# Expert weights split tile by tile inside the attention loop, padding rows written by plain transfers

## The chip, the cores and the metric

The kernel runs on one core of a Trainium2 chip. The metric is the time of one execution on the device in microseconds (us), taken as the median of the runs. TensorE is called PE, VectorE DVE, ScalarE ACT, GpSimd POOL and SyncE SP, as in the profile. SP does nothing here but issue transfers.

## What is computed

One decoder layer on x, 2048 rows by 256 columns, all in float32:

```python
x = x + attn(_layernorm(x))      # one head of width 256; scores q A q^T / 16, softmax, times v, times the row's norm
x = x + xattn(_layernorm(x), ctx, mask)   # 4 heads of 64, 1601 context rows
x = x + ffn(_layernorm(x))       # 4 experts of 256 -> 1024 -> 256 with exact GELU

idx = argmax(softmax(x @ Wg + bg))        # each row goes to one expert
out = gelu(x @ W1[idx] + b1[idx]) @ W2[idx] + b2[idx]
```

## The kernel before

**Precision.** Each float32 operand of a large product is held as a high half (rounded to the matmul's type) and a low half (the rest), and three matmuls (high by high, high by low, low by high) replace one. ACT makes the high half by a copy, DVE the low half by a subtraction (`low`, line 1316). Nearly every PSUM tile in the kernel goes through such a pair. The expert weights W1 and W2 (4 MB each) need it too.

**Prologue** (to about 95 us): keys and values of both attentions are made and stay in SBUF, in `keys_self`, `vals_self`, `keys_cross` and `vals_cross`.

**Attention loop.** The 2048 rows are T = 16 tiles of 128 rows. All engines run the same pipelined pass `body(j, k)`, 18 times (`run_pipeline`, line 400): in pass j, part a works on the self-attention of tile j, part b on the first cross-attention heads of tile j-1, and part c on the last heads, the output projection, the gate and the routing of tile j-2. Passes 3 to 14 are one hardware loop; passes 0 to 2 and 15 to 17 are written out. Pass 16 (k = T) has no part a, and pass 17 (k = T+1) has only part c. The order within each engine is written by hand in `body`, and semaphores tie the engines together. PE's three PSUM banks for transposes are handed from one use to the next in a fixed order.

**Routing.** For each tile DVE finds the expert and the place of every row (`gates`, `ranks`, `destination`), and POOL scatters the tile's records (256 columns and the row's number) into `rows_dram` by an indirect transfer (line 631). `rows_dram` has one region of 2048 + 128 records for each expert. Expert blocks are 128 records, so behind the last record of each expert there must be padding records. In pass 17, after `pad_rows` (line 1657, DVE) has worked out where each expert's records end so far, POOL issues eight indirect transfers of 128 padding records each (lines 599 to 607), two for each expert, and the last record scatter waits for them (line 630).

**Weights.** After the last x1 SP loads W1 and then W2, in eight pieces of 1 MB, through two halves of `w_stage` (lines 486 to 501). ACT makes the high half (`weights_hi`, line 1145) and DVE the low half (`weights_lo`, line 1451) of each piece, four of them in pass 16, two in pass 17, and two behind it. `w1s` and `w2s` lie in SBUF where the keys and values lay, so none of it can begin before those are done with.

**Experts.** DVE works out a table of the 19 blocks, which says for each where its rows and weights lie (lines 1721 to 1744). Then SP loads 128 records (`load_rows`), DVE and POOL normalise them, PE multiplies with W1, DVE adds b1, ACT applies GELU, PE multiplies with W2, DVE adds b2 and x, and POOL scatters the rows to the output, 19 times (`blocks`). Columns of the weights are chosen by a register loaded from the table.

Of the kernel before, what the change touches and what calls it, by code (L numbers as in the profile page):

```python
# [46 lines left out]
NOBODY = 65536.0  # L47

# [29 lines left out]
def emit(nc, io, ctx):  # L78
# [8 lines left out]
    rows_dram = nc.dram_tensor("rows_dram", [XROWS, REC], F32, kind="Internal").ap()  # L87

# [29 lines left out]
    pad_f = sb("pad_f", [P, 2, E], F32)  # L118
    pad_i = sb("pad_i", [P, 2, E], U32)
# [3 lines left out]
    tab = sb("tab", [P, 5, BLOCKS], F32)  # L123
    table = sb("table", [P, 3, BLOCKS], I32)
# [71 lines left out]
    ps_self = sb("ps_self", [P, 4, 2, 512], F32R, loop)  # L196
# [10 lines left out]
    o_tile = sb("o_tile", [P, H, HD], F32, loop)  # L207
    ot = sb("ot", [P, 2, C, P], F32R, loop)
    xn3 = sb("xn3", [P, D], F32, loop)
    x3t = sb("x3t", [P, C, P], F32, loop)  # L210
# [139 lines left out]
    pad_dest = sem("pad_dest")  # L350
    pad_dest_i = sem("pad_dest_i")
# [3 lines left out]
    w_loaded = [sem("w_loaded_even"), sem("w_loaded_odd")]  # L355
    b_loaded = sem("b_loaded")
    w_hi = sem("w_hi")
    w_lo = sem("w_lo")
# [62 lines left out]
    def _(sp):  # L421
# [42 lines left out]

        loads_a(0)
# [15 lines left out]

        sp.wait_ge(x1_ready, T)
        for n in range(2 * E):
            e = n % E
            if n >= 2:
                sp.wait_ge(w_hi, n - 1)
                sp.wait_ge(w_lo, n - 1)  # L490
            if n < E:
                sp.dma_start(w_stage[:, n % 2, :].rearrange("p (c n) -> p c n", c=C),
                             io["W1"][e].rearrange("(c p) n -> p c n", p=P)).then_inc(w_loaded[n % 2], 16)
            else:
                sp.dma_start(w_stage[:, n % 2, :].rearrange("p (c n) -> p c n", c=FC),
                             io["W2"][e].rearrange("(c p) n -> p c n", p=P)).then_inc(w_loaded[n % 2], 16)
            if n == E + 1:

                sp.wait_ge(cross_p_used, 16 * T)
                sp.dma_start(b2_row[:, :], bass.AP(io["b2"].tensor, 0, [[0, P], [1, E * D]])).then_inc(b_loaded, 16)  # L500
                sp.dma_start(b1_row[:, :], bass.AP(io["b1"].tensor, 0, [[0, P], [1, E * DF]])).then_inc(b_loaded, 16)

        sp.wait_ge(spare_stored, 16 * E)
        sp.wait_ge(routed, 16 * T)
        sp.wait_ge(table_ready, 3)
# [23 lines left out]
    def _(pool):  # L529
# [50 lines left out]
        def body(j, k):  # L580
# [18 lines left out]
            if k == T + 1:  # L599


                for n in range(2):
                    for e in range(E):
                        pool.wait_ge(pad_dest_i, 1)
                        pool.indirect_dma_start(out=rows_dram[:, :],  # L605
                                                out_offset=bass.IndirectOffsetOnAxis(ap=pad_i[:, n, e:e + 1], axis=0),
                                                in_=pads[:, :], in_offset=None).then_inc(pads_out, 16)
# [12 lines left out]
            if c:  # L620
# [8 lines left out]
                if k == T + 1:  # L629
                    pool.wait_ge(pads_out, 16 * 2 * E)  # L630
# [35 lines left out]
    def _(pe):  # L666
# [99 lines left out]
        def self_values(j, k, g):  # L766
            pe.wait_ge(self_p_lo, 4 * j + g + 1)
            for n in range(4):
                m = 4 * g + n
                for a, b in ((0, 0), (0, 1), (1, 0)):  # L770
                    mm = pe.matmul(self_out[:, 0:D], ps_self[:, g, a, n * P:(n + 1) * P], vals_self[:, m, b, :],  # L771
# [255 lines left out]
        pe.wait_ge(table_ready, 3)  # L1027
# [8 lines left out]
        def blocks(b, k):  # L1036
# [10 lines left out]
            if k < BLOCKS:  # L1047
                if k == 0:
                    pe.wait_ge(w_lo, E)
                pe.wait_ge(f_xt_lo, b + 1)  # L1050
                off = pe.value_load(table[0:1, 1, bass.ds(b, 1)], min_val=0, max_val=(E - 1) * DF)
                for n in range(2):
                    three(scores[:, n, :], lambda a, c: xt_f[:, a, c, :],
                          lambda p, c: w1s[:, p, c, bass.ds(off + n * 512, 512)]).then_inc(f_h, 1)
            if k < BLOCKS - 1:
                flip_x(b + 1, k + 1)
            if k >= 1:
                if k == 1:
                    pe.wait_ge(w_lo, 2 * E)
                off2 = pe.value_load(table[0:1, 2, bass.ds(b - 1, 1)], min_val=0, max_val=(E - 1) * D)  # L1060
                if k >= 2:
                    pe.wait_ge(f_out, b - 1)
                for f in range(FC):
                    if f % 4 == 0:
                        pe.wait_ge(f_ht_lo, 2 * (b - 1) + f // 4 + 1)
                    for a, p in ((0, 0), (0, 1), (1, 0)):
                        mm = pe.matmul(cross_out[:, 0:D], ht[:, a, f, :], w2s[:, p, f, bass.ds(off2, D)],  # L1067
# [6 lines left out]
    def _(act):  # L1074
# [70 lines left out]
        def weights_hi(n):  # L1145

            e = n % E
            act.wait_ge(w_loaded[n % 2], 16 * (n // 2 + 1))
            if n < E:
                copy(w1s[:, 0, :, e * DF:(e + 1) * DF], w_stage[:, n % 2, :].rearrange("p (c n) -> p c n", c=C)).then_inc(w_hi, 1)  # L1150
# [23 lines left out]
        def body(j, k):  # L1174
# [11 lines left out]
            if k == T:  # L1186
                weights_hi(0)
# [669 lines left out]
```

## Time and profile before

| | us |
|---|---|
| three runs | 841.83, 843.74, 843.75 |
| median | 843.74 |
| span of the profiled execution | 848.8 |
| its time outside the span | not shown by the profile |
| PE busy in the span | 755.1 (89%) |
| DVE | 653.2 (77%) |
| ACT | 457.9 (54%) |
| POOL | 138.9 (16%) |

The span is the time from the first to the last instruction of one profiled execution; it is 5 us longer than the median of the runs without a profile. Busy time of an engine is the sum of its instructions' times. A wait is shown as idle time in front of an instruction, with the one whose signal ended it. The granted clock of PE is given as a share of 2.4 GHz, so 1.00 is 2.4 and 0.50 is 1.2 GHz. In the profile a line such as L1318 can be that of a helper: L1318 is every low half, L1076 every copy on ACT. The loop's passes are 33.9 us apart. The drain passes 16 and 17 lie at 620 to 662 and 662 to 694 us, and the expert blocks from 700 us to the end, 6.73 us apart.

### The profile page before, as it was taken

What the parts mean: (1) busy time and instruction counts of PE and PEld (TensorE: products, weight loads), DVE (VectorE), ACT (ScalarE), POOL (GpSimd) and SP (SyncE); (2) the same over time, 40 slices, a digit from 0 to 9 for tenths busy, and PEclk for the clock granted to TensorE, in tenths of its full rate; (3) what the DMA queues carried; (4) which work ended last, traced back from release to release, by engine and by line L of the source; (5) the groups of instructions that cost most, each with busy time, mean ns of one, the idle gap of its engine ahead of it and who ended that gap; (6) DMA issues with size and microseconds to landing.
All of it is one profiled execution on the core that took longest, in us unless ns stands there. A gap on an engine that the chain in (4) does not pass through costs nothing. (4 is left out here: it accounts for less than half of the span.)

```text
span 848.8 us, 19493 instructions
## 1 busy us (share of the span) xinstructions
PE 755.1 (89%) x6136; PEld 681.1 (80%) x6137; DVE 653.2 (77%) x1619; ACT 457.9 (54%) x922; POOL 138.9 (16%) x246
## 2 busy tenths in 40 slices
PE   3988799999999999999999999999986416999996
PEld 2778689989889899898898998988975314999995
DVE  5984647788888888888888888888878465777773
ACT  2544626566566665666666656666665432334332
POOL 3100110120211201202112012021120410222221
PEclk9999989999999999999999999999978856999999
DMA  6242110010101000000010000000123260111110
GB/s 211 70 138 70 47 29 7 24 29 15 29 12 28 28 6 28 24 16 28 12 28 28 6 28 24 17 28 12 54 113 99 101 235 26 36 39 39 37 33 15
DMA packets 25525, 39.32 MB, mean 46 GB/s; under 512 B 3086, under 2 KB 18704, under 8 KB 25360
## 3 DMA queue, kind: packets, MB, share of 16 engines
q1 hardware_dynamic: 23232, 33.02, 12.5%
q0 software_dynamic: 2256, 5.83, 2.0%
q8 instruction: 21, 0.34, 0.2%
q14 instruction: 16, 0.13, 0.0%
HBM read 28.82 MB, written 10.41 MB: 46 GB/s over the span
## 5 line engine op out<-in xcount | busy, mean ns | idle before, releaser
L1076 ACT ACTIVATE ps_cross<-flip 128x512 f16<-128x512 f32 (+1 forms) x256 | 125.0, 514 | 116.5 <-PE flip L795 91.0
L1318 DVE TENSOR_TENSOR ps_cross<-flip,ps_cross 128x512 f16<-128x512 f32 (+1 forms) x256 | 145.0, 583 | 24.8 <-ACT ps_cross L1076 20.4
L795 PE MATMUL flip<-ident,exp_cross 128*128 128x128 f32 (+1 forms) x832 | 131.8, 282 | 9.9 <-DVE ps_cross L1318 6.5
L1277 ACT ACTIVATE exp_cross<-exp_cross,xneg 128x1024 f32<-128x1024 f32 (+1 forms) x128 | 122.7, 960 | 19.2 <-DVE xneg L1492 19.1
L784 PE MATMUL scores<-keys_cross,qt 128*128 128x402 f32 x512 | 127.6, 372 | 5.3 <-DVE xneg L1492 3.5
L795 PEld LDWEIGHTS flip<-ident,exp_cross 128*128 128x128 f32 (+1 forms) x832 | 95.8, 143 | 18.1 <-DVE ps_cross L1318 8.3
L672 PE MATMUL scores<-keys_self,u_tile 128*128 128x512 f32 x384 | 102.2, 403 | 6.4 <-issue 4.9
L806 PE MATMUL cross_out<-vals_cross,ps_cross 128*128 128x128 f16 (+1 forms) x832 | 102.5, 224 | 5.5 <-issue 4.9
L771 PE MATMUL flip<-vals_self,ps_self 128*128 128x256 f32 x768 | 103.8, 289 | 0.0
L806 PEld LDWEIGHTS cross_out<-vals_cross,ps_cross 128*128 128x128 f16 (+1 forms) x832 | 76.4, 101 | 28.3 <-issue 20.4
L771 PEld LDWEIGHTS flip<-vals_self,ps_self 128*128 128x128 f32 x768 | 96.7, 194 | 0.0
L808 PE MATMUL cross_out<-vals_cross,ps_cross 128*128 128x64 f16 (+1 forms) x832 | 95.6, 195 | 0.0
L784 PEld LDWEIGHTS scores<-keys_cross,qt 128*128 128x128 f32 x512 | 87.4, 193 | 5.8 <-DVE xneg L1492 3.6
L672 PEld LDWEIGHTS scores<-keys_self,u_tile 128*128 128x128 f32 x384 | 67.6, 188 | 19.2 <-issue 6.0
L808 PEld LDWEIGHTS cross_out<-vals_cross,ps_cross 128*128 128x128 f16 (+1 forms) x832 | 75.1, 100 | 1.1
L1492 DVE CUSTOM_DVE_ANT_0 exp_cross<-scores,mask_bias,xneg 128x804 f32<-128x804 f32 x64 | 67.3, 1052 | 7.5 <-PE scores L784 4.2
L1492 DVE CUSTOM_DVE_ANT_0 exp_cross<-scores,mask_bias 128x804 f32<-128x804 f32 x64 | 63.3, 988 | 4.2 <-PE scores L784 2.6
L672 PE MATMUL scores<-w1s,xt_f 128*128 x228 | 61.6, 421 | 2.4 <-issue 2.4
L1067 PE MATMUL cross_out<-w2s,ht 128*128 x456 | 58.2, 284 | 1.2 <-DVE ht L1318 1.2
L1067 PEld LDWEIGHTS cross_out<-w2s,ht 128*128 128x128 f32 x456 | 54.9, 189 | 1.5 <-issue 1.4
L672 PEld LDWEIGHTS scores<-w1s,xt_f 128*128 128x128 f32 x228 | 43.9, 200 | 12.6 <-issue 3.0
L1076 ACT ACTIVATE ps_self<-flip 128x512 fp32r<-128x512 f32 x64 | 38.6, 605 | 28.3 <-PE flip L763 28.2
(207 smaller groups left out, 1189.2 us busy)
## 6 DMA issues: line engine op xcount, KB each, us to landing
w_stage<-W SPq DMA_DIRECT2D x8, 1024.0 KB, 5.4
u_dram<-u_out SPq DMA_DIRECT2D x4, 1024.0 KB, 5.9
u_tile<-u_dram SPq DMA_DIRECT2D x16, 256.0 KB, 2.7
mask_tile<-mask SPq DMA_DIRECT2D x16, 200.1 KB, 2.4
rows<-rows_dram SPq DMA_DIRECT2D x19, 130.0 KB, 2.1
x_all<-x SPq DMA_DIRECT2D x4, 512.0 KB, 5.8
x_tile<-x SPq DMA_DIRECT2D x16, 128.0 KB, 2.0
b_row<-b SPq DMA_DIRECT2D x1, 2048.0 KB, 8.9
```

What stands on the lines that cost most here:

```text
L672: mm = pe.matmul(out, lhs(a, c), rhs(b, c), start=(n == 0 and first), stop=(n == 3 * C - 1 and last))
L771: mm = pe.matmul(self_out[:, 0:D], ps_self[:, g, a, n * P:(n + 1) * P], vals_self[:, m, b, :], start=(m == 0 and a == 0 and b == 0), stop= ...
L784: mm = pe.matmul(scores[:, n, 0:KB], qt[:, h, :], keys_cross[:, part, h, n * KB:(n + 1) * KB], start=(part == 0), stop=(part == 1))
L795: tr = pe.transpose(flip[0:rows, bank(use), n * P:(n + 1) * P], exp_cross[:, h % 2, m * P:m * P + rows], ident[:, :])
L806: pe.matmul(cross_out[:, h * P:(h + 1) * P], ps_cross[0:rows, g, 0, n * P:(n + 1) * P], vals_cross[0:rows, m, h, :, :], start=(m == 0), st ...
L808: mm = pe.matmul(cross_out[:, h * P:h * P + HD], ps_cross[0:rows, g, 1, n * P:(n + 1) * P], vals_cross[0:rows, m, h, 0, :], start=False, s ...
L1067: mm = pe.matmul(cross_out[:, 0:D], ht[:, a, f, :], w2s[:, p, f, bass.ds(off2, D)], start=(f == 0 and a == 0 and p == 0), stop=(f == FC - ...
L1076: return act.activation(out, in_, ACT.Copy, **kw)
L1277: act.activation(exp_cross[:, h % 2, cols], exp_cross[:, h % 2, cols], ACT.Exp, bias=xneg[:, h % 2, 1:2], scale=-1.0, accum_out=xden[:, ha ...
L1318: return dve.tensor_tensor(out, full, hi, ALU.subtract)
L1492: dve.tensor_tensor_reduce(exp_cross[:, h % 2, cols].rearrange("p (n s) -> p n s", n=2), scores[:, 2 * half:2 * half + 2, 0:KB], mask_bias ...
```

## The change

1. **Weights in the loop.** In each of the 16 passes with part a, SP loads one sixteenth of W1 and of W2 (256 KB each) into `w_piece`. ACT copies it to `w_high`, POOL subtracts that from `w_piece` in place, and SP stores the four tiles (256 KB each) to `w1_dram` and `w2_dram`. At the end SP loads the finished halves, 16 MB in 16 transfers, straight into `w1s` and `w2s`. `weights_hi`, `weights_lo` and `w_stage` are gone.
2. **Padding.** For each tile t SP writes padding records over block t of all four regions by one plain transfer (and over the 17th at the end), before any record of a tile can be placed there. The record scatter of a tile waits for the padding of blocks that it may reach. `pad_rows` and the eight indirect transfers are gone.
3. **Room.** `ps_self` has three buffers for its four groups, `o_tile` and `x3t` share the memory of `qs`, and `ot` that of `xt`.
4. **Table.** A third column pair gives one offset for `w1s` and `w2s` alike, since the weights of an expert now lie together.

```diff
-    w1s = sb("w1s", [P, 2, C, E * DF], F32R, ffn)
-    w2s = sb("w2s", [P, 2, FC, E * D], F32R, ffn)
-    w_stage = sb("w_stage", [P, 2, C * DF], F32, ffn)
+    w1s = sb("w1s", [P, E * WE], F32R, ffn)
+    w2s = sb("w2s", [P, E * WE], F32R, ffn)
...
-    ps_self = sb("ps_self", [P, 4, 2, 512], F32R, loop)
+    ps_self = sb("ps_self", [P, 3, 2, 512], F32R, loop)
+    w_piece = sb("w_piece", [P, 2, 512], F32R, loop)
+    w_high = sb("w_high", [P, 2, 512], F32R, loop)
...
+        def load_piece(t):
+            sp.dma_start(w_piece[:, 0, :].bitcast(F32), w1_pieces[bass.ds(t, 1), :, :].rearrange("a p f -> p (a f)")).then_inc(piece_loaded, 16)
+            sp.dma_start(w_piece[:, 1, :].bitcast(F32).rearrange("p (r d) -> p r d", r=2),
+                         w2_pieces[bass.ds(t, 1), :, :, :].rearrange("a p r d -> p (a r) d")).then_inc(piece_loaded, 16)
+
+        def keep_piece(t):
+            for part, held in ((0, w_high), (1, w_piece)):
+                sp.dma_start(w1_dram[part, bass.ds(t, 1), :, :].rearrange("a p f -> p (a f)"), held[:, 0, :].bitcast(F32)).then_inc(piece_kept, 16)
+                sp.dma_start(w2_dram[part, bass.ds(t, 1), :, :].rearrange("a p f -> p (a f)"), held[:, 1, :].bitcast(F32)).then_inc(piece_kept, 16)
...
+        def pad_block(t):
+            sp.wait_ge(pads_out, 16 * t)
+            sp.dma_start(regions[bass.ds(t, 1), :, :, :].rearrange("a p e c -> p (a e) c"),
+                         pads[:, :].unsqueeze(1).broadcast_to([P, E, REC])).then_inc(pads_out, 16)
...
         sp.wait_ge(prologue_done, 3)
         loads_m(0)
+        load_piece(0)
+        sp.wait_ge(padding_set, 4)
 
         def body(j, k):
...
             if k < T - 1:
                 sp.wait_ge(scores_ready, 4 * j + 4)
                 loads_a(j + 1)
+            if k < T:
+
+                sp.wait_ge(piece_hi, j + 1)
+                sp.wait_ge(piece_lo, j + 1)
+                keep_piece(j)
+                if k >= 1:
+                    pad_block(j)
+                else:
+                    first_pads()
+            if k < T - 1:
                 sp.wait_ge(x1_ready, j + 1)
                 loads_x(j + 1)
+                sp.wait_ge(piece_kept, 64 * (j + 1))
+                load_piece(j + 1)
...
+        pad_block(T)
+        sp.wait_ge(piece_kept, 64 * T)
+        sp.wait_ge(scores_ready, 4 * T)
+        load_w1(0)
+        load_w1(1)
         sp.wait_ge(x1_ready, T)
...
+        load_w1(2)
+        load_w1(3)
+        sp.dma_start(b1_row[:, :], bass.AP(io["b1"].tensor, 0, [[0, P], [1, E * DF]])).then_inc(b_loaded, 16)
+        sp.dma_start(b2_row[:, :], bass.AP(io["b2"].tensor, 0, [[0, P], [1, E * D]])).then_inc(b_loaded, 16)
+        sp.wait_ge(cross_scores_ready, 8 * T)
+        for e in range(E - 1):
+            load_w2(e)
+        sp.wait_ge(cross_p_used, 16 * T)
+        load_w2(E - 1)
...
             if a:
 
                 if b:
                     pool.wait_ge(coef_step, 2 * j)
                 pool.tensor_copy(norm_col[:, :], norms[:, bass.ds(j, 1)]).wait_op(constants_set, CONSTANTS, "sem-ge").then_inc(norm_ready, 1)
+            if a:
+
+                pool.wait_ge(piece_hi, j + 1)
+                pool.tensor_tensor(w_piece[:, :, :], w_piece[:, :, :].bitcast(F32), w_high[:, :, :].bitcast(F32),
+                                   ALU.subtract).then_inc(piece_lo, 1)
...
+                pool.wait_ge(pads_out, 16 * (j - 1))
                 pool.indirect_dma_start(out=rows_dram[:, :], out_offset=bass.IndirectOffsetOnAxis(ap=dest_i[:, 0:1], axis=0),
...
-            if k == T:
-                weights_hi(0)
+            if a:
+                piece_high(j)
             if b:
                 act.wait_ge(q_ready, j)
...
+            if g == 3:
+                act.wait_ge(self_p_used, 4 * j + 1)
+            elif k >= 1:
+                act.wait_ge(self_p_used, 4 * j if g == 0 else 4 * j + g - 3)
...
+        for n, width in ((1, DF), (2, D), (3, WE)):
+            step(dve.tensor_scalar(tab[:, 3 + n, :], tab[:, 0, :], float(E - 1), float(width), ALU.min, ALU.mult))
+            dve.tensor_copy(table[:, n, :], tab[:, 3 + n, :]).then_inc(table_ready, 1)
+        dve.wait_ge(table_ready, 4)
```

Here `WE` is 4096, `load_w1` and `load_w2` issue one transfer of 1 MB for each half of one expert's weights, and `piece_high` is ACT's copy of `w_piece` to `w_high` behind the wait for `piece_loaded`.

## Rows read from the trace of the kernel before

**Rows 1.** Busy time by stretch: stretch, length, PE, PEld, DVE, ACT, POOL, granted clock, DMA, GB/s.
```profile
400.00:500.00 100.00, 98.42 (x899) 89.33 (x899) 85.61 (x223) 62.91 (x135) 15.16 (x27) 1.00 0.07 22
...
620.30:662.20 41.90, 28.38 (x217) 24.37 (x216) 31.66 (x66) 24.81 (x42) 6.73 (x10) 0.80 0.24 79
662.20:693.90 31.70, 11.08 (x88) 8.76 (x86) 16.33 (x48) 10.77 (x17) 11.01 (x13) 0.64 0.56 195
```

**Rows 2.** Timeline of PE in pass 16: start, us, instruction, [idle before, releaser].
```profile
629.11 1.09 PE L826 MATMUL flip<-ident,qs 128*128 128x128 f32 x4 [1.71 <-DVE qs L1318]
...
640.55 1.71 PE L784 MATMUL scores<-keys_cross,qt 128*128 128x402 f32 x4 [3.46 <-DVE xneg L1492]
...
654.48 0.66 PE L795 MATMUL flip<-ident,exp_cross 128*128 128x128 f32 x4 [1.66 <-DVE ps_cross L1318]
...
662.08 0.16 PE L835 MATMUL flip<-onehot,below 128*128 128x4 bf16 x1 [2.75 <-DVE onehot L1692]
```

**Rows 3.** Instructions on w_stage: count, ns min/median/max, first and last start.
```profile
L1076 ACT ACTIVATE w1s<-w_stage x4: 1899/1903/1905, 624.4 to 657.0; 128x2048 fp32r<-128x2048 f32 x4
L1318 DVE TENSOR_TENSOR w1s<-w_stage,w1s x4: 2291/2292/2294, 626.3 to 658.9; 128x2048 fp32r<-128x2048 f32 x4
```

**Rows 4.** Timelines of PE, ACT, POOL and DVE in pass 17, in order of time.
```profile
673.69 0.30 PE L795 MATMUL flip<-ident,exp_cross 128*65 128x128 f32 x1
...
677.76 0.27 ACT L1076 ACTIVATE ps_cross<-flip 65x128 f16<-65x128 f32 x1 [4.46 <-remote]
...
678.00 0.96 POOL L605 DMA_INDIRECT rows_dram<-pads,pad_i  x1 [0.31 <-issue]
...
678.49 0.26 PE L808 MATMUL cross_out<-vals_cross,ps_cross 65*128 65x64 f16 x1
...
680.66 0.69 DVE L1552 TENSOR_REDUCE o_tile<-cross_out 128x256 f32<-128x512 f32 x1 [2.31 <-remote]
```

**Rows 5.** Timeline of POOL: the power for rs3 in passes 15 and 17.
```profile
609.41 0.57 POOL L615 TENSOR_TENSOR rs<-rs,minus_half 128x1 f32<-128x1 f32 x1 [12.93 <-DVE rs L1589]
...
686.83 1.48 POOL L615 TENSOR_TENSOR rs<-rs,minus_half 128x1 f32<-128x1 f32 x1 [7.86 <-DVE rs L1589]
```

**Rows 6.** Timelines of POOL and DVE from the last scatter to the first expert block.
```profile
694.69 1.05 POOL L631 DMA_INDIRECT rows_dram<-record,dest_i  x1 [5.88 <-DVE dest_i L1707]
...
697.52 0.18 DVE L1743 CAST table<-tab 128x19 int32<-128x19 f32 x1
...
705.58 4.48 DVE L1318 TENSOR_TENSOR w2s<-w_stage,w2s 128x2048 fp32r<-128x2048 f32 x2
...
712.56 1.29 DVE L1795 TENSOR_TENSOR hidden<-scores,b_row 128x512 f32<-128x512 f32 x2 [0.61 <-PE scores L672]
```

**Rows 7.** Line 631, the record scatters: time from issue to landing over all 16.
```profile
DMA to landing us min/median/max: 2.6/2.6/3.6
```

**Rows 8.** Timeline of one loop tile, all engines, in order of time.
```profile
491.76 0.39 ACT L1076 ACTIVATE qs<-flip 128x256 fp32r<-128x256 f32 x1 [2.05 <-PE flip L672]
...
492.80 1.53 POOL L598 TENSOR_SCALAR mask_bias<-mask_tile 128x1601 bf16<-128x1601 uint8 x1
...
493.88 0.46 DVE L1528 TENSOR_TENSOR xcoef<-xden 128x4 f32<-128x4 f32 x1
...
494.39 0.19 POOL L612 COPY norm_col<-norms 128x1 f32 x1
...
494.58 0.23 DVE L1532 TENSOR_SCALAR xcoef<-xcoef,v_scale 128x4 f32<-128x4 f32 x1
...
495.46 0.10 PEld L806 LDWEIGHTS cross_out<-vals_cross,ps_cross 128*128 128x128 f16 x1 [0.19 <-DVE ps_cross L1318]
```

**Rows 9.** DMA issues of the page: count, KB each, us to landing.
```profile
w_stage<-W SPq DMA_DIRECT2D x8, 1024.0 KB, 5.4
...
u_tile<-u_dram SPq DMA_DIRECT2D x16, 256.0 KB, 2.7
```

**Rows 10.** Instructions on xcoef: count, ns min/median/max, first and last start.
```profile
L1528 DVE TENSOR_TENSOR xcoef<-xden x16: 148/450/840, 154.2 to 667.9; 128x4 f32<-128x4 f32 x16
```

More of the change, by code:

```diff
@@ L47 @@
 NOBODY = 65536.0
+WE = 2 * C * DF
 NG = -(-MC // 4)
@@ L206, in emit @@
     qt = sb("qt", [P, H, P], F32R, loop)
-    o_tile = sb("o_tile", [P, H, HD], F32, loop)
-    ot = sb("ot", [P, 2, C, P], F32R, loop)
+    o_tile = qs[:, 0:2, :, :].bitcast(F32).rearrange("p a two d -> p (a two) d")
+    ot = xt
     xn3 = sb("xn3", [P, D], F32, loop)
-    x3t = sb("x3t", [P, C, P], F32, loop)
+    x3t = qs[:, 2:4, :, :].bitcast(F32).rearrange("p c two d -> p c (two d)")
     bs1 = sb("bs1", [P, 6], F32, loop)
@@ L486, in _ @@
[L486 to L501, printed above, removed]
+        w1_parts = w1_dram.rearrange("two (e c q) (r s) f -> two e c (q r) (s f)", e=E, c=C, s=2)
@@ new lines, in _, with load_w1, load_w2 @@
+        w2_parts = w2_dram.rearrange("two (e q) p f -> two e q p f", e=E)
+        def load_w1(e):
+            whole = w1s[:, e * WE:(e + 1) * WE].bitcast(F32).rearrange("p (two c f) -> p two c f", two=2, c=C)
+            for part in range(2):
+                sp.dma_start(whole[:, part, :, :], w1_parts[part, e, :, :, :].rearrange("c p f -> p c f")).then_inc(w1_loaded, 16)
+        def load_w2(e):
+            whole = w2s[:, e * WE:(e + 1) * WE].bitcast(F32).rearrange("p (two q f) -> p two q f", two=2, q=4)
+            for part in range(2):
+                sp.dma_start(whole[:, part, :, :], w2_parts[part, e, :, :, :].rearrange("q p f -> p q f")).then_inc(w2_loaded, 16)
@@ L770, in self_values @@
                 for a, b in ((0, 0), (0, 1), (1, 0)):
-                    mm = pe.matmul(self_out[:, 0:D], ps_self[:, g, a, n * P:(n + 1) * P], vals_self[:, m, b, :],
+                    mm = pe.matmul(self_out[:, 0:D], ps_self[:, g % 3, a, n * P:(n + 1) * P], vals_self[:, m, b, :],
                                    start=(m == 0 and a == 0 and b == 0), stop=(m == T - 1 and a == 1))
@@ L1066, in blocks @@
                     for a, p in ((0, 0), (0, 1), (1, 0)):
-                        mm = pe.matmul(cross_out[:, 0:D], ht[:, a, f, :], w2s[:, p, f, bass.ds(off2, D)],
+                        mm = pe.matmul(cross_out[:, 0:D], ht[:, a, f, :], w2s[:, bass.ds(off2 + (p * FC + f) * D, D)],
                                        start=(f == 0 and a == 0 and p == 0), stop=(f == FC - 1 and a == 1))
@@ L1143, in _, with piece_high @@
         act.wait_ge(prologue_done, 3)
[L1145 to L1150, printed above, removed]
-            else:
-                act.wait_ge(cross_p_used, 16 * T)
-                copy(w2s[:, 0, :, e * D:(e + 1) * D], w_stage[:, n % 2, :].rearrange("p (c n) -> p c n", c=FC)).then_inc(w_hi, 1)
+        def piece_high(j):
+            act.wait_ge(piece_loaded, 32 * (j + 1))
+            copy(w_high[:, :, :], w_piece[:, :, :].bitcast(F32)).then_inc(piece_hi, 1)
         def cross_hi(j, k, h, g):
@@ L1282, in _ @@
         copy(barrier[:, 0:1], ident[:, 0:1]).then_inc(attention_done, 1)
-        for n in (E + 2, E + 3):
-            weights_hi(n)
         act.wait_ge(attention_done, 3)
@@ L1449, in _ @@
         dve.wait_ge(prologue_done, 3)
-        def weights_lo(n, part=None):
-            e = n % E
-            dve.wait_ge(w_hi, n + 1)
-            if n < E:
-                w, cols, ch = w1s, slice(e * DF, (e + 1) * DF), C
-            else:
-                w, cols, ch = w2s, slice(e * D, (e + 1) * D), FC
-            at = slice(0, ch) if part is None else slice(part * ch // 2, (part + 1) * ch // 2)
-            op = low(w[:, 1, at, cols], w_stage[:, n % 2, :].rearrange("p (c n) -> p c n", c=ch)[:, at, :],
-                     w[:, 0, at, cols].bitcast(F32))
-            if part != 0:
-                op.then_inc(w_lo, 1)
         def cross_lo(j, k, h, g):
@@ L1655, in body @@
                 destination(j, k)
-        def pad_rows():
-            dve.wait_ge(rank_used, T - 1)
-            for n in range(2):
-                dve.tensor_scalar(pad_f[:, n, :], seen[:, :], lane[:, 0:1], float(n * P), ALU.add, ALU.add).then_inc(pad_dest, 1)
-            dve.wait_ge(pad_dest, 2)
-            dve.tensor_copy(pad_i[:, :, :], pad_f[:, :, :]).then_inc(pad_dest_i, 1)
         def gates(j, k, part):
@@ L1779, in blocks @@
                 x_lo_f(0)
-                for n in range(E + 2, 2 * E):
-                    weights_lo(n)
                 statistics(b + 1, 1)
```

87 lines of the change are left out of this document (25 added, 62 removed).

## The prediction

> **What bounds the kernel now.** I read first the busy time by stage [rows 1]. In the attention loop (one slice of it: 400 to 500 us) PE is busy 98.4 us of 100 at a granted clock of 1.00, DVE 86, ACT 63, POOL 15: the loop is bound by PE, and work on ACT, POOL or the DMA queues is free there as long as PE and DVE meet no new wait. After the loop's tiles come two drain passes, k = 16 (620.3 to 662.2 us) and k = 17 (662.2 to 693.9). PE is busy 28.4 of 41.9 us and 11.1 of 31.7 us in them, at clocks of 0.80 and 0.64. So they are chains of waits, and what stands on the chain there costs its full length. The expert blocks that follow are bound by PE again and the change leaves their matmuls alone. So I look for gains between 620 and 716 us, and for losses in the loop.
>
> **Splitting the weights in pass 16 (removed).** Four pairs of an ACT copy and a DVE subtraction of 128x2048 sit in DVE's and ACT's order. The timeline of PE shows who waits: 1.71 us for qs, 3.46 for xneg, 1.66 for ps_cross and 2.75 for onehot, each in front of a matmul and each right after one of the four subtractions [rows 2]. Their sum is 9.6 us. About 0.3 of the first remains, since qs needs its own copy and subtraction anyway: 9.3. From above the price is bounded by the whole work, 4 x 1.90 us on ACT and then 4 x 2.29 on DVE [rows 3], 16.8; from below by the two waits in which DVE was plainly behind a subtraction that PE did not need (3.46 and 2.75), 6.2. I take 9.3, as PE's idle time is the measure that sits on the chain.
>
> **The eight padding transfers in pass 17 (removed).** POOL issues them one after another at 1.27 us each, the last at 678.00 [rows 4]. POOL itself is not on the chain: it is next needed for rs3, at 686.83 [rows 5]. But while they run, two signals of PE reach the others late. PE's transpose starts at 673.69 and takes 0.30 us, yet ACT's copy of it starts at 677.76: 3.7 us lost. PE's last matmul of the value sum ends at 678.75, yet DVE's o_tile starts at 680.66 (ACT and SP, which wait for the same count, start then too): 1.9 us lost [rows 4]. The profile puts both down to "remote", and has such a wait nowhere else in the span. I take it that the burst of indirect transfers holds them up, because they coincide and because no other scatter in the loop has one: 5.6 us. Bounds: nothing (a coincidence) and 5.6. The forecast takes 5.6, and the other end is a rival.
>
> **Smaller terms.** POOL's power for rs3 in pass 17, started at 686.83 beside one of DVE's subtractions for W2, takes 1.48 us where it takes 0.57 in a loop tile [rows 5]; DVE's xn3 waits for it: 0.9 gained. In the first expert block, the subtractions of the last two W2 pieces hold DVE for 4.48 us from 705.58, so that the first bias addition starts at 712.56 [rows 6] though the first half of its matmuls was done some 3 us before; without them only the second half's addition is on the chain, at 712.2 at the earliest, and ends at 712.9 instead of 713.85. With the transposed x then split earlier too I take 1.3 (bounds 0.4 and 2). The last record scatter starts at 694.69 [rows 6] and took the longest of all landings, 3.6 us against 2.6 in the median [rows 7]: landed at 698.3, and then SP loads the first rows. A quiet queue would land it at 697.3, but the table, whose last cast starts at 697.52 [rows 6], now has a third pair of steps. Two more steps of 0.18 less one wait put its end at 697.9. So 0.4 gained, not 1.0 (bounds 0 and 0.4).
>
> **What the loop gets.** Per tile: on ACT a copy of 128x1024, on POOL a subtraction of the same size, on SP two loads (512 KB), four stores (1 MB) and the padding write (0.5 MB).
> - ACT: from the row of 128x2048 at 1.90 us [rows 3], half the size is about 1.0 us. It stands before the copy of qs, in front of which ACT is idle 2.05 us [rows 8]: hidden; without that cover it would cost 1.0 per tile.
> - POOL: no row has a subtraction of two full inputs. Below: a one-input row, 1.53 us for 1601 elements [rows 8], so 0.98 for 1024. Above, no row bounds it but the 12.93 us for which POOL is idle before rs3 [rows 5], beyond which it would delay rs3. I take twice the one-input price, 2.0 us. Either end is free as far as POOL goes.
> - DMA: a 256 KB load lands in 2.7 us and a 1024 KB one in 5.4 [rows 9]: 3.5 us per MB. 2 MB more per tile of 33.9 us is 7 us of transfers. They go out after the next scores tile is requested and after x1, when nothing of the tile's chain is in flight; the record scatter, which POOL does wait for, falls between. SP's own queue: about eight more issues of 0.33 us, and its waits for POOL's subtraction stand in front of only the x load, which goes out 12 us later anyway.
> - Three buffers for four groups of ps_self: group 3 now waits for the values of group 0, which stand before its transposes in PE's own order: nothing. The shared buffers of qs, xt, o_tile and x3t are dead when they are reused: nothing.
> - Start: in pass 0 the first piece is loaded after the prologue's barrier and copied before ACT's first exponential, and in pass 1 it can be asked for only after x1 of pass 0, a few us before ACT comes to it. Some 2.7 for a load and 1.0 for a copy stand against PE's scores for the tile, which ACT waits for anyway. I charge 0.5 (bounds 0 and 3.7).
>
> **Loading the halves.** 18.5 MB now go to SBUF between about 605 and the first W2 matmul, where it was 10.5. At 3.5 us per MB, W1 and the biases (10.5 MB) are there by 642, and W2 (8 MB, 6 of them from the last cross scores, near 652 in the new order) by 682. The first W2 matmul would be near 703. Twenty us of room: free, unless the rate falls below 0.6 of these rows.
>
> **Sum.** 9.3 + 5.6 + 0.9 + 1.3 + 0.4 - 0.5 = 17.0 us. The profiled span is 848.8 us (its own time outside the span isn't shown) and the median of the runs 843.74, 5 us less; a difference carries over, so 848.8 - 17.0 = 831.8 for the span and 843.7 - 17.0 = 826.7 for the runs. I say 827.0. Terms at their poor ends except the stalls give 13; at their good ends 22: 822 to 831.
>
> **Where POOL and DVE meet: a rule against the change.** In the tile read, DVE's addition for xcoef starts at 493.88 and ends as POOL's mask_bias ends, at 494.33 [rows 8]; over all tiles it takes 0.148 us at the least, 0.450 in the median and 0.840 at the most [rows 10]. So the two engines do exclude each other on some pairs of instructions. Next on DVE comes the scaling of xcoef, at 494.58, while POOL's norm_col ends at that moment and the new 2.0 us subtraction would start some 0.07 later [rows 8]. If DVE's scaling falls behind it, DVE stands about 1.8 us, and PE, which waits for DVE's next subtraction at 495.46 with 0.19 us idle already [rows 8], stands with it. The Trainium skill (SBUF — State Buffer, "Who interferes with whom") says that a DVE instruction with two SBUF inputs contends with a GpSimd instruction that reads SBUF, that tensor_scalar can take a mode that uses the shared ports, and that the first to start blocks the other for its whole length. By that rule the gain hangs on those 0.07 us; the trace agrees with its first half by that addition's 0.148 to 0.840 us, and no row here shows the second.
>
> **Rivals.**
> - *The signals stay late.* The 5.6 us were not the padding transfers': another 11.4 gained, so 832.3 (829 to 836). For it: nothing in the trace ties PE's signal to POOL but the time. Chance 0.22.
> - *DVE is shut out by POOL's subtraction.* 14 tiles (k from 2 to 15) by 1.8 us is 25 us lost: 843.7 - 17 + 25 = 852, slower. It decides at the scaling of xcoef: if it starts later than POOL's subtraction. Against it: DVE is first by the rows, and both are released by the same mask_bias, so their order should repeat. Chance 0.11.
> - *The halves come late.* At half the measured rate W1 and biases end near 680, W2 near 736, which holds the first W2 matmul by some 30 us: 857. The rows show 1 MB transfers at full rate beside others. Chance 0.03.
> - *The stalls of pass 16 belong to its chain.* If PE's waits there only change their name, what is left is a few us and the start eats part of it: about 842. Against it: the loop runs the same chain with PE never idle. Chance 0.04.
>
> **Numbers.** The forecast has 0.60. A difference under 0.3% (2.5 us) can't be told from no change here. Faster: 0.60 + 0.22 + half of the last rival, 0.84; same 0.02; slower 0.14. The range takes the forecast's own 822 to 831 and the first rival's up to 836, with 1.5 us of margin below: 820.5 to 836.
>
> **What would show it.** In the new profile PE's idle time of pass 16 should be near 4 us instead of 13.5 and the pass near 32 us; pass 17 near 25; no "remote" wait; ACT's new copy in front of qs with no PE wait behind it; the DVE scaling of xcoef still 0.23 us and starting within 0.3 us of the end of mask_bias; tiles still 33.9 us apart; W2 landed before its first matmul. I am wrong if the tiles are further apart, if a wait for w1s or w2s appears on PE, or if the late signals are still there.

## The result and the profile after

The changed kernel takes 873.31 us (median of 4 runs, 869.48 to 875.33) against 843.75 for the kernel before: a ratio of 1.035, 95% interval 1.032 to 1.038, 29.6 us slower. The forecast was 827.0 (820.5 to 836), and 873 also lies beyond the 852 of the rival in which DVE is shut out.

The page of the kernel after: the span, the busy time of each engine, and PE's value matmuls. They wait 28.2 us for DVE's subtractions; in the kernel before that wait was 0.2 us in its second profile (experiment 6).

```profile
span 873.6 us, 19805 instructions
PE 767.2 (88%) x6136; PEld 692.5 (79%) x6137; DVE 665.9 (76%) x1608; ACT 461.4 (53%) x930; POOL 165.2 (19%) x254
L856 PE MATMUL cross_out<-vals_cross,ps_cross 128*128 128x128 f16 (+1 forms) x832 | 105.3, 228 | 28.3 <-DVE ps_cross L1351 28.2
```

Busy time by stretch of the kernel after, with the columns of [rows 1]: a slice of the loop, two stretches of one tile each to compare, and passes 16 and 17.

```profile
400.00:500.00 100.00, 92.09 (x800) 82.81 (x798) 83.26 (x200) 60.37 (x123) 21.49 (x29) 0.95 0.25 82
...
490.00:528.00 38.00, 35.30 (x314) 32.04 (x311) 31.78 (x76) 22.68 (x46) 7.63 (x11) 0.96 0.22 75
566.00:602.00 36.00, 33.34 (x305) 30.20 (x304) 31.35 (x76) 22.43 (x47) 7.23 (x11) 1.00 0.24 79
...
668.30:699.30 31.00, 23.34 (x218) 19.84 (x217) 22.82 (x62) 17.52 (x37) 5.19 (x10) 0.94 0.44 179
699.30:723.60 24.30, 11.75 (x90) 9.53 (x88) 10.84 (x34) 7.66 (x16) 2.38 (x5) 0.64 0.98 351
```

Pass 16 is 11 us shorter than in [rows 1] and pass 17 is 7 us shorter. (Of these 7 at most 1 is a gain: without the late signals of that one profile pass 17 takes 25.2 and 24.2 us in experiments 6 and 7, and 24.3 here.) What is gained is outweighed in the loop. PE was busy 98.4 us of 100 there and is busy 92.1, at a clock of 0.95. The tiles are 37.7 us apart instead of 33.9 in twelve periods (about 37.6 to 37.8) and 36.1 apart in one: 47 us in all.

What a tile looks like now, in the timeline of all engines (start, us, instruction, idle before and releaser). It answers to [rows 8]:

```profile
301.24 1.53 POOL L653 TENSOR_SCALAR mask_bias<-mask_tile 128x1601 bf16<-128x1601 uint8 x1
...
302.27 0.50 DVE L1543 TENSOR_TENSOR xcoef<-xden 128x4 f32<-128x4 f32 x1
...
302.81 0.18 DVE L1545 RECIPROCAL xcoef<-xcoef 128x4 f32<-128x4 f32 x1
302.82 0.19 POOL L658 COPY norm_col<-norms 128x1 f32 x1
...
302.97 2.35 POOL L662 TENSOR_TENSOR w_piece<-w_piece,w_high 128x1024 fp32r<-128x1024 f32 x1
303.02 2.32 DVE L1547 TENSOR_SCALAR xcoef<-xcoef,v_scale 128x4 f32<-128x4 f32 x1
...
305.26 1.87 DVE L1351 TENSOR_TENSOR ps_cross<-flip,ps_cross 128x512 f16<-128x512 f32 x3
...
306.00 0.23 PE L856 MATMUL cross_out<-vals_cross,ps_cross 128*128 128x128 f16 x1 [2.10 <-DVE ps_cross L1351]
```

DVE's scaling of 4 elements per partition takes 2.32 us where it took 0.23: it starts 0.05 us after POOL's subtraction and ends with it. So it is in 13 tiles (k from 3 to 15); in pass 2 the scaling comes 3.6 us after the subtraction's start and keeps its 0.23 us. DVE's next subtraction is late by as much, and PE stands 2.10 us. That is the second rival. The windows behind the wait show a second cost:

```profile
302.00:305.00 3.00, 1.90 (x29) 1.65 (x26) 2.90 (x5) 3.00 (x7) 2.94 (x3) 1.00 0.36 81
305.00:308.00 3.00, 2.00 (x16) 1.88 (x17) 2.35 (x5) 1.10 (x3) 0.32 (x1) 0.82 0.77 278
308.00:311.00 3.00, 3.00 (x22) 2.75 (x21) 1.77 (x5) 1.47 (x3) 0.00 (x0) 0.61 0.93 324
311.00:314.00 3.00, 3.00 (x31) 2.82 (x29) 2.85 (x5) 1.84 (x3) 0.00 (x0) 1.00 0.00 0
```

After the wait the granted clock drops from 1.00 to 0.82 and 0.61 before it is back, with PE busy throughout the second of these windows. So 2.1 us of the 3.8 are the wait, and the other 1.7 are matmuls at the lower level, 1.2 GHz: 3 x (1 - 0.82) + 3 x (1 - 0.61) = 1.7 us of full speed missing in the two windows. The one short period, the tile at 566 us, has the same scaling (2.33 us) and the same wait (2.13 us), but its clock stays at 1.00, and it costs 2.2 us instead of 3.8. Why it is spared isn't known. The same stretch carries the piece's stores, so the trace alone leaves open whether the transfers slow the tile as well.

### The profile page after: what moved, and what is told of

It is laid out like the page before. It is cut to its first block and busy times, and to the rows that moved or that the text cites. A ratio compares the mean times of both kernels' runs of the same rounds, so it can differ in the third digit from the quotient of the medians.

```text
span 873.6 us, 19805 instructions
## 1 busy us (share of the span) xinstructions
PE 767.2 (88%) x6136; PEld 692.5 (79%) x6137; DVE 665.9 (76%) x1608; ACT 461.4 (53%) x930; POOL 165.2 (19%) x254
## 5 line engine op out<-in xcount | busy, mean ns | idle before, releaser
L834 PE MATMUL scores<-keys_cross,qt 128*128 128x402 f32 x512 | 133.3, 385 | 4.3 <-DVE xneg L1511 2.3
L856 PE MATMUL cross_out<-vals_cross,ps_cross 128*128 128x128 f16 (+1 forms) x832 | 105.3, 228 | 28.3 <-DVE ps_cross L1351 28.2
L856 PEld LDWEIGHTS cross_out<-vals_cross,ps_cross 128*128 128x128 f16 (+1 forms) x832 | 78.5, 104 | 51.9 <-DVE ps_cross L1351 36.5
L858 PE MATMUL cross_out<-vals_cross,ps_cross 128*128 128x64 f16 (+1 forms) x832 | 98.2, 198 | 0.0
L834 PEld LDWEIGHTS scores<-keys_cross,qt 128*128 128x128 f32 x512 | 91.9, 203 | 5.0 <-DVE xneg L1511 2.7
L858 PEld LDWEIGHTS cross_out<-vals_cross,ps_cross 128*128 128x128 f16 (+1 forms) x832 | 76.9, 101 | 1.6
L722 PE MATMUL scores<-w1s,xt_f 128*128 x228 | 59.6, 411 | 2.6 <-issue 2.6
L1351 DVE TENSOR_TENSOR ps_self<-flip,ps_self 128x512 fp32r<-128x512 f32 x64 | 44.1, 691 | 22.1 <-ACT ps_self L1126 21.9
```

The costliest lines, as they stand in the source:

```text
L722: mm = pe.matmul(out, lhs(a, c), rhs(b, c), start=(n == 0 and first), stop=(n == 3 * C - 1 and last))
L834: mm = pe.matmul(scores[:, n, 0:KB], qt[:, h, :], keys_cross[:, part, h, n * KB:(n + 1) * KB], start=(part == 0), stop=(part == 1))
L856: pe.matmul(cross_out[:, h * P:(h + 1) * P], ps_cross[0:rows, g, 0, n * P:(n + 1) * P], vals_cross[0:rows, m, h, :, :], start=(m == 0), st ...
L858: mm = pe.matmul(cross_out[:, h * P:h * P + HD], ps_cross[0:rows, g, 1, n * P:(n + 1) * P], vals_cross[0:rows, m, h, 0, :], start=False, s ...
L1351: return dve.tensor_tensor(out, full, hi, ALU.subtract)
```

## The experiments

**1. The subtraction after DVE's scaling.** POOL waits for the scaling before it subtracts. Nothing else is touched.

```diff
                 pool.wait_ge(piece_hi, j + 1)
+                if c:
+                    pool.wait_ge(o_step, 3 * (j - 1))
                 pool.tensor_tensor(w_piece[:, :, :], w_piece[:, :, :].bitcast(F32), w_high[:, :, :].bitcast(F32),
```

> The changed kernel, but POOL waits for DVE's third coefficient step of the tile, the scaling of xcoef, before it subtracts the weight piece. Nothing else moves, all transfers are as in the changed kernel. Theory 1, POOL's subtraction locks DVE's scaling out: the scaling goes from 2.32 us back to 0.23, PE loses its wait of about 2.1 us per tile and its stretch at half clock behind it, tiles go from 37.7 to 33.9 us apart in 13 passes, 47 us less: 873.3 - 47 = 826 us (823 to 830). Theory 2, the 2 MB more of transfers per tile slow the loop: nothing changes, 870 to 875 us. Theory 3, the late place of the subtraction delays POOL's next steps or the piece's stores: the scaling is short, but another wait of over 0.5 us per tile appears, 833 us or more.

Measured: 826.3 us (824.6 to 827.1), ratio to before 0.978 (0.976 to 0.980). The same tile in its timeline, and two of its windows:

```profile
290.35 0.18 DVE L1547 RECIPROCAL xcoef<-xcoef 128x4 f32<-128x4 f32 x1
290.37 0.19 POOL L658 COPY norm_col<-norms 128x1 f32 x1
290.56 0.23 DVE L1549 TENSOR_SCALAR xcoef<-xcoef,v_scale 128x4 f32<-128x4 f32 x1
290.70 0.68 DVE L1353 TENSOR_TENSOR ps_cross<-flip,ps_cross 128x512 f16<-128x512 f32 x1
290.88 2.37 POOL L664 TENSOR_TENSOR w_piece<-w_piece,w_high 128x1024 fp32r<-128x1024 f32 x1 [0.32 <-DVE xcoef L1549]
292.09 1.29 DVE L1353 TENSOR_TENSOR ps_cross<-flip,ps_cross 128x512 f16<-128x512 f32 x2 [0.71 <-ACT ps_cross L1128]
```

```profile
400.00:500.00 100.00, 98.20 (x898) 89.02 (x897) 85.59 (x221) 65.55 (x137) 22.30 (x30) 1.00 0.24 77
620.80:651.70 30.90, 23.37 (x219) 19.68 (x217) 22.75 (x62) 17.42 (x37) 5.21 (x10) 0.94 0.58 234
```

The whole loss is gone with all transfers still there (DMA share 0.24 in the loop, 0.25 in the changed kernel): theory 1. No granted clock below 1.00 is left behind the scaling in any of the 13 tiles. Note what DVE does beside the 2.37 us of POOL: subtractions that take one input from PSUM, at their usual time, 0.68 us for one and 1.29 for two. Not all of DVE is shut out, only some of its instructions. This version beats both kernels.

**2 and 3. The length of the subtraction.** The same place, over fewer columns; the low halves of the other columns are left out.

```diff
-                pool.tensor_tensor(w_piece[:, :, :], w_piece[:, :, :].bitcast(F32), w_high[:, :, :].bitcast(F32),
+                pool.tensor_tensor(w_piece[:, :, 0:1], w_piece[:, :, 0:1].bitcast(F32), w_high[:, :, 0:1].bitcast(F32),
```

(in the second of them 0:256 for 0:1)

> The changed kernel, but POOL subtracts one column of 512 in each half of the weight piece (the rest of the low halves is left out, so the weights stay less exact); the place of the instruction and all transfers stay. Theory 1 (lock): the subtraction takes about 0.1 us, so the lock is over before it costs anything: scaling 0.23 us or at most 0.3, tiles 33.9 us apart, about 826 us (823 to 830), the same as with the late subtraction within 3 us. Theory 2 (transfers): tiles stay 37.7 us apart, 870 us or more.

> The changed kernel, but POOL subtracts 256 of 512 columns in each half of the weight piece (half of the low halves is left out). Theory 1 (lock, as long as POOL's instruction): the subtraction takes 1.2 us, DVE's scaling 1.2, PE's wait per tile falls by the same 1.15 us, from 2.1 to 0.95. If the half clock behind the wait comes with every wait in proportion, tiles are 33.9 + 3.8 x 0.95/2.1 = 35.6 us apart and the time is 826 + 13 x 1.7 = 848 us; if the clock does not fall after a wait that short, 34.9 us and 839 us. Theory 2 (transfers): 37.7 us and 870 or more.

Measured: 828.9 us (827.9 to 831.5) with one column, 841.9 (839.9 to 845.3) with half. The instructions on xcoef (count, ns min/median/max, first and last start): first with one column, together with POOL's subtraction of one tile from the timeline, then with half.

```profile
L1547 DVE TENSOR_SCALAR xcoef<-xcoef,v_scale x16: 229/229/232, 155.2 to 659.9; 128x4 f32<-128x4 f32 x16
```

```profile
291.44 0.20 POOL L662 TENSOR_TENSOR w_piece<-w_piece,w_high 128x2 fp32r<-128x2 f32 x1
```

```profile
L1547 DVE TENSOR_SCALAR xcoef<-xcoef,v_scale x16: 229/1247/1252, 153.7 to 671.4; 128x4 f32<-128x4 f32 x16
```

A tile with half the columns, in the timeline, and its windows behind the wait:

```profile
292.96 1.27 POOL L662 TENSOR_TENSOR w_piece<-w_piece,w_high 128x512 fp32r<-128x512 f32 x1
293.01 1.25 DVE L1547 TENSOR_SCALAR xcoef<-xcoef,v_scale 128x4 f32<-128x4 f32 x1
...
294.91 0.23 PE L856 MATMUL cross_out<-vals_cross,ps_cross 128*128 128x128 f16 x1 [1.04 <-DVE ps_cross L1351]
```

```profile
295.00:298.00 3.00, 3.00 (x32) 2.94 (x32) 2.56 (x5) 2.11 (x5) 0.00 (x0) 1.00 0.93 341
298.00:301.00 3.00, 3.00 (x30) 2.66 (x29) 2.95 (x7) 1.79 (x3) 0.00 (x0) 1.00 0.74 258
```

The scaling follows POOL's subtraction, which starts 0.05 us before it each time: 2.32 us beside 2.35, 1.25 beside 1.27, and its own 0.23 beside 0.20. The wait on PE follows too, 2.10 and 1.04 us in the tiles shown. But the time does not follow in proportion: after the shorter wait (0.84 to 1.24 us over the tiles) the clock stays at 1.00 in all 13 tiles, and a tile costs 1.0 us more than in experiment 1 (35.06 apart instead of 34.03), after 2.10 it costs 3.7 more in twelve of the 13. 13 periods by 1.03 are 13.4, and 826.3 + 13.4 = 839.7. The measured 841.9 is 2 above that, which stays open, and 6 below the 848 of a proportional fall of the clock; the windows decide for the case without one. With one column the time is 2.6 above experiment 1, of which 1.5 is a pace of the expert blocks that experiment 7 comes to; the tiles are 34.1 us apart.

**4. Who is first.** One more copy of a single column on POOL, ahead of the subtraction. No new wait on another engine.

```diff
+                if b:
+                    pool.wait_ge(idle_done, j)
+                pool.tensor_copy(idle_col[:, :], minus_half[:, 0:1]).wait_op(constants_set, CONSTANTS, "sem-ge").then_inc(idle_done, 1)
                 pool.wait_ge(piece_hi, j + 1)
```

> The changed kernel with one more small copy (one column) on POOL between norm_col and the subtraction, which then starts about 0.2 us later, at about 0.15 us after DVE's scaling of xcoef instead of 0.05 before it; nothing waits for anything new. Theory 1, whichever of the two starts first shuts the other out: DVE's scaling takes 0.23 us, POOL's subtraction starts a little later or takes 0.1 longer, tiles are 34.0 us apart, 826 us (824 to 830). Theory 2, the subtraction slows any DVE work beside it in proportion to the overlap, whoever is first: the instructions of DVE behind the scaling take the 2.1 us, tiles 37 us or more apart, 860 to 875 us.

Measured: 826.6 us (824.7 to 826.9), ratio 0.979 (0.977 to 0.981). Its timeline:

```profile
287.59 0.19 POOL L660 COPY norm_col<-norms 128x1 f32 x1
287.71 0.19 POOL L664 COPY idle_col<-minus_half 128x1 f32<-128x1 f32 x1
287.79 0.23 DVE L1552 TENSOR_SCALAR xcoef<-xcoef,v_scale 128x4 f32<-128x4 f32 x1
287.86 2.40 POOL L667 TENSOR_TENSOR w_piece<-w_piece,w_high 128x1024 fp32r<-128x1024 f32 x1
```

DVE is first by 0.07 us now, as the prediction had expected of the plain change, and keeps its 0.23 us. In the changed kernel POOL is first by 0.05. The 0.12 us between the two cost 47 us of kernel time. POOL's instruction still runs beside the last 0.16 us of the scaling and beside DVE's work behind it, at no cost to the tile (34.03 us apart, as in experiment 1). So it is not the overlap that costs: the order decides.

The Trainium skill (SBUF — State Buffer, "Who interferes with whom") says of DVE instructions in the modes that use the shared ports that whoever issues first gets them for the whole instruction and the other fully blocks. The runs agree where POOL is first: 2.32 us beside 2.35, 1.25 beside 1.27. Where DVE is first they show that it keeps its 0.23 us; that POOL is blocked meanwhile they hardly show (2.40 us against 2.37 in experiment 1, with 0.16 us of overlap), and no run shows in which mode the scaling runs.

**5. The padding alone.** The kernel before with a plain transfer per tile; the eight indirect transfers and the DVE and POOL steps for them are gone.

```diff
             if k < T - 1:
                 sp.wait_ge(scores_ready, 4 * j + 4)
                 loads_a(j + 1)
+            if k < T:
+                if k >= 1:
+                    pad_block(j)
+                else:
+                    first_pads()
...
-            if k == T + 1:
-                for n in range(2):
-                    for e in range(E):
-                        pool.wait_ge(pad_dest_i, 1)
-                        pool.indirect_dma_start(out=rows_dram[:, :],
-                                                out_offset=bass.IndirectOffsetOnAxis(ap=pad_i[:, n, e:e + 1], axis=0),
-                                                in_=pads[:, :], in_offset=None).then_inc(pads_out, 16)
```

> The kernel before with the padding part of the change alone: one plain transfer per tile writes the padding rows, the eight indirect transfers and what computes their addresses are gone; the weights are still split after the loop. Theory 1, the burst of indirect transfers holds up PE's signals: the two late signals of pass 17 (3.7 and 1.9 us) are gone, 843.7 - 5.6 = 838.1 us (836.5 to 840). Theory 2, the signals are late for another reason: they stay, 842.5 to 844 us. If only the first is the transfers', 840 us.

Measured: 844.6 us (841.6 to 846.6, 12 runs) against 843.1 for before (22 runs), ratio 1.001 (0.9995 to 1.0022). The padding part alone brings nothing. Its profile shows gains all the same: 2.3 us between the count of the records and the first W2 product, and 0.65 at the very end. Against them stands the loop: from pass 2 to pass 15, measured at the same DVE step (the cast of onehot), it takes 442.3 to 442.6 us in experiments 1, 2, 4 and 5, which have the plain transfers, and 441.2 to 441.9 in the kernel before and in experiments 6, 7 and 8, which do not. That is some 1 us; where the rest goes was not traced.

**6. The kernel before, once more,** unchanged, for a second profile.

> The kernel before, unchanged, for a second profile. Theory 1, the eight indirect transfers of pass 17 hold up PE's signals each time: a transpose's copy and the sum over o_tile are late again by 3.7 and 1.9 us, the span is 848 us or more. Theory 2, the late signals belonged to that one execution: pass 17 takes 24 to 25 us instead of 30.9, the span is 840 to 843 us.

Its span is 844.9 us, 3.9 less than that of the first profile, and in neither of the two forecast ranges. Its pass 17 in the timeline of PE, ACT, DVE and POOL, the rows that answer to [rows 4]:

```profile
674.78 0.30 PE L795 MATMUL flip<-ident,exp_cross 128*65 128x128 f32 x1
674.92 0.96 POOL L605 DMA_INDIRECT rows_dram<-pads,pad_i  x1 [0.30 <-issue]
675.12 0.27 ACT L1076 ACTIVATE ps_cross<-flip 65x128 f16<-65x128 f32 x1 [0.85 <-PE flip L795]
...
675.84 0.19 PE L808 MATMUL cross_out<-vals_cross,ps_cross 65*128 65x64 f16 x1
676.07 0.69 DVE L1552 TENSOR_REDUCE o_tile<-cross_out 128x256 f32<-128x512 f32 x1 [0.35 <-PE cross_out L808]
```

```profile
620.40:663.00 42.60, 27.79 (x220) 23.99 (x218) 31.81 (x66) 25.07 (x42) 6.72 (x10) 0.84 0.22 78
663.00:688.20 25.20, 12.11 (x88) 10.02 (x88) 16.04 (x41) 10.65 (x17) 10.98 (x13) 0.60 0.64 227
```

The same burst of indirect transfers runs, and ACT's copy starts 0.34 us after the transpose, not 4.1. Pass 17 takes 25.2 us instead of 31.7. The late signals belonged to one execution. What caused them there stays open. So does a surplus of this second one: it took 846.85 us, 3.2 above the median of the seven other runs of that round (843.68, the highest 844.25), without any late signal.

**7. The layout of W2.** In the changed kernel the product with W2 took 2.74 us per block in the chain of waits against 2.83 before. This is the kernel before with only W2's halves laid out by expert.

```diff
-    w2s = sb("w2s", [P, 2, FC, E * D], F32R, ffn)
+    w2s = sb("w2s", [P, E * 2 * FC * D], F32R, ffn)
...
-                        mm = pe.matmul(cross_out[:, 0:D], ht[:, a, f, :], w2s[:, p, f, bass.ds(off2, D)],
+                        mm = pe.matmul(cross_out[:, 0:D], ht[:, a, f, :], w2s[:, bass.ds(off2 + (p * FC + f) * D, D)],
```

> The kernel before with W2's halves laid out in SBUF by expert, high and low side by side, as the changed kernel has them, and nothing else. Theory 1, the place of W2's rows in SBUF sets the speed of PE's reads: the 24 matmuls of a block take 2.74 us instead of 2.83 and the 19 blocks 1.7 to 2 us less, 841.9 us. Theory 2, the 0.09 us per block of the changed kernel come from something else (what DVE or the queues do beside it): 2.83 us stay, 843.7 us.

Measured: 843.75 us (12 runs), ratio 1.0006 (0.9993 to 1.0019): the layout is worth nothing. The blocks are 6.73 us apart in this run and 6.63 in experiments 1, 3 and 4, but 6.72 in experiment 2, which runs the same code there as 3. So two paces exist, about 1.5 us apart over the 19 blocks, and what selects them stays open. This run too has the eight indirect transfers and no late signal: its pass 17 takes 24.2 us.

**8. The fourth corner.** Experiment 1 with the old padding: no plain transfers, the eight indirect ones back in pass 17. The other three corners are before, experiment 5 and experiment 1.

```diff
+            if k == T + 1:
+                for n in range(2):
+                    for e in range(E):
+                        pool.wait_ge(pad_dest_i, 1)
+                        pool.indirect_dma_start(out=rows_dram[:, :],
+                                                out_offset=bass.IndirectOffsetOnAxis(ap=pad_i[:, n, e:e + 1], axis=0),
+                                                in_=pads[:, :], in_offset=None).then_inc(pads_out, 16)
...
-                if k >= 1:
-                    pad_block(j)
-                else:
-                    first_pads()
```

> The kernel with the late subtraction (826.3 us), but the padding rows are written as in the kernel before: eight indirect transfers in pass 17, no plain transfer per tile. It is the other half of the square whose corners are before (844.3), before with plain padding (844.6) and this change with the late subtraction (826.3). Theory 1, the burst of indirect transfers holds up PE's signals in pass 17: 826.3 + 5.6 = 832 us, with a wait on PE of about 3.7 us in pass 17. Theory 2, the padding part is worth nothing anywhere: 826.3, within 1.5. Theory 3, plain padding is worth the 2.3 us between the count and the first W2 matmul and the 0.65 us at the end by which before with plain padding was shorter there: 829 us.

Measured: 832.5 us (830.7 to 832.8), ratio 0.987 (0.985 to 0.989), 6.2 more than experiment 1. The number is that of theory 1, the mechanism is not. Timeline of POOL and DVE at the last rs3:

```profile
669.53 0.15 DVE L1601 TENSOR_SCALAR rs<-mv 128x1 f32<-128x1 f32 x1
...
672.05 0.96 POOL L647 DMA_INDIRECT rows_dram<-pads,pad_i  x1 [0.30 <-issue]
673.04 0.59 POOL L664 TENSOR_TENSOR rs<-rs,minus_half 128x1 f32<-128x1 f32 x1
...
673.67 0.41 DVE L1615 TENSOR_SCALAR xn<-record,mv,rs 128x256 f32<-128x256 f32 x1 [3.98 <-POOL rs L664]
```

And the same place in experiment 1:

```profile
669.49 0.15 DVE L1602 TENSOR_SCALAR rs<-mv 128x1 f32<-128x1 f32 x1
669.73 0.57 POOL L668 TENSOR_TENSOR rs<-rs,minus_half 128x1 f32<-128x1 f32 x1 [7.42 <-DVE rs L1602]
...
670.34 0.41 DVE L1616 TENSOR_SCALAR xn<-record,mv,rs 128x256 f32<-128x256 f32 x1 [0.70 <-POOL rs L668]
```

No signal of PE is late. POOL is still issuing padding when rs3 is due, and the chain waits 3.3 us for it. In the kernel before POOL had 7.86 us of idle time at this place [rows 5]: there rs3 was due later, with W2's splitting still in front of it. Of the other 2.9 us, 1.4 are the slower pace of the blocks, which experiment 2 has with plain padding too, so it can't be put down to the padding. And 0.65 lie at the end (6.68 us from the start of the last W2 matmul to the end of the span against 6.03, in all profiled kernels with the indirect padding against all without); the rest was not traced.

| | old padding | plain padding |
|---|---|---|
| weights split after the loop | 1 (before) | 1.001 (0.9995 to 1.0022) |
| weights split in the loop, subtraction late | 0.987 (0.985 to 0.989) | 0.978 (0.976 to 0.980) |

## Why the prediction was wrong

**The step that failed** stands in "Where POOL and DVE meet": the new subtraction "would start some 0.07 later", so that DVE's scaling would be first. I had put POOL's next start 0.07 us behind the end of norm_col (494.39 + 0.19 + 0.07 = 494.65 against DVE's 494.58). In the trace after, the subtraction starts 0.15 us after the start of norm_col (302.82, 302.97), before that copy's shown end at 303.01. With 0.15 the sum is 494.54, ahead of DVE. The trace of before had such overlaps. Just ahead of the rows that were read, in the same tile, a copy starts 0.04 us before the shown end of the power ahead of it, and it does so in 14 of 14 tiles:

```profile
486.91 0.55 POOL L619 TENSOR_TENSOR rs<-rs,minus_half 128x1 f32<-128x1 f32 x1 [12.74 <-DVE rs L1648]
487.42 0.19 POOL L624 COPY record<-token 128x1 f32<-128x1 f32 x1
```

The other POOL instructions of that tile that wait for no other engine start 0.06 to 0.16 us behind the end of the one before them. So the rows of before allowed both orders. The mechanism and the place that decides were named, and experiment 4 shows that the decision was as narrow as the rows said. What was wrong was to give 0.11 to a side of a 0.07 us margin when the start of an instruction that the trace did not contain was known no better than to 0.1. It was near an even chance with 47 us at stake (873.3 against 826.3).

**The rival's price** was low by half: 1.8 us per tile against 3.8, 852 against 873, although it counted 14 tiles and 13 are hit. The subtraction takes 2.35 us instead of 2.0, which gives a wait of 2.1, and the clock's fall adds 1.7, which I had not counted at all. Experiment 3 shows the two apart: 1.0 us per tile for a wait of 1.0.

With the order put right (experiment 1) the kernel takes 826.3 us where 827.0 was forecast. That the sum fits so well is luck: its largest term was right only in part, and the second largest was not there. The 22 us of its good end don't come out of the terms either: they give 18.2 with the 9.3 of pass 16 kept, and 25.7 with its 16.8. Term by term:
- *Pass 16*, 9.3 forecast: 41.9 us before, 31.0 and 30.9 after, so 11 gained, 1.7 more than forecast. But PE's idle time in it falls from 13.5 only to 7.5 us (30.9 - 23.4, experiment 1), not to 4. The other 5.0 are PE's own work, 28.4 us before and 23.4 now at a granted clock of 0.94 instead of 0.80, a term that the sum did not have. The largest of the four waits mostly stays, with no weight subtraction in the pass; it was 3.46 us [rows 2], and in experiment 1 it is:

```profile
634.99 0.99 PE L836 MATMUL scores<-keys_cross,qt 128*128 128x402 f32 x4 [2.53 <-DVE xneg L1513]
```

- *The late signals*, 5.6: nothing. Experiment 5 took the transfers away and gained nothing, experiment 6 kept them and had no late signal. The hint was in the table ahead of the prediction: the profiled span was 5 us above the median of the runs, while for every later kernel it was 1.7 to 2.1 us below its own execution's time. By that it took some 851 us itself, 7 above the median; the 5.6 us were part of this surplus, and they could not be gained from the median. "A difference carries over" was wrong for this term.
- *The padding transfers*: once the weights are out of the way, the kernel with the old padding takes 6.2 us more. 3.3 of them come by another mechanism: POOL is held, not PE's signals (experiment 8). I had written that POOL is not on the chain, which was true only of the chain of before. 0.65 more go with the padding, and 1.4 are a pace of the blocks that was not forecast and whose cause is open. These three stand, by luck, where the phantom 5.6 stood.
- *rs3 in pass 17*, 0.9: right, 0.57 us after instead of 1.48. Experiment 5, which still splits W2 there but has no indirect transfers, keeps 1.48, and experiment 8, with the transfers and without W2's subtractions, has 0.59: so DVE's subtraction was the cause, as I had written.
- *First block and landing*, 1.7: from the count of the records to the first W2 product it takes 22.5 us in experiment 1 and 22.8 in the changed kernel, against 26.4 and 27.3 in the two profiles of before: some 4 gained, 2.3 of them with the padding alone (24.1 in experiment 5).
- *The start*, 0.5: not to be told apart. The first x1 starts at 115.1 and 115.6 in the two profiles of before, and between 112.9 and 116.1 in the changed kernels.
- *Loading the halves* and *DMA in the loop*: free, as forecast. No wait of PE for w1s or w2s shows; in experiment 1 the last half of W1 has landed at 633.6 us and the last of W2 at 676.0, 22 us before its first product, where 642, 682 and 20 had been estimated. And the tiles there are 34.03 us apart against 33.96 and 33.94 in the two profiles of before.

## What to carry to other kernels

Before work is moved to POOL, list every DVE instruction with only SBUF operands that can start within a few tenths of a microsecond of it, and fix their order with a semaphore when a PE wait hangs on it: here one such wait turned 3.5% slower into 2.2% faster. When a margin is that small, read from the trace how soon that engine starts its next instruction in several places, not in one. Price a new wait on PE with what the clock does behind it, not only with its own length. And compare the profiled span with the runs before a wait that occurs once is put into a sum; where two parts of a change free the same stretch, cost the second with the first already done.

## What the runs showed of the hardware

- DVE's scaling of 4 elements per partition lasts 0.23 us alone and as long as POOL's two-input instruction, within 0.03 us, if that starts as little as 0.05 us earlier (1.25 beside 1.27, 2.32 beside 2.35 us). If DVE starts 0.07 us earlier, it keeps 0.23 us and POOL takes 2.40. DVE's subtractions with an input in PSUM keep their 0.68 us beside it.
- A PE wait of 2.1 us was followed by a lower granted clock in 12 of 13 tiles (0.82 and 0.61 in two windows of 3 us in the one shown), at a cost of 1.7 us, and by none in the tile at 566 us; waits of 0.84 to 1.24 us were followed by no fall in 13 tiles.
- POOL's subtraction of two 128x1024 inputs takes 2.35 us, of 128x512 1.27 us, against 1.53 us for one input of 128x1601.
- POOL's subtraction started 0.15 us after the start of a one-column copy and 0.04 before that copy's shown end (302.82 + 0.19 against 302.97).
- POOL issued indirect transfers of 128 rows 1.27 us apart, and ran nothing else between them: eight of them held a power of 128x1 by 3.3 us (experiment 8).
